# Attention pipeline of a transformer block: three batches' cross and self passes in 32 shared slots

## The reference, cut to what matters

```python
x = x + self_attention(norm(x))      # 16 heads, 4 key heads, width 32, ALiBi, window and global tokens masked out
x = x + cross_attention(norm(x), ctx, ctx)   # 32 heads, 8 key heads, width 16, keys = values = ctx
x = x + moe(norm(x))                 # 32 experts, top 4 of 2 groups, capacity 128, plus a shared expert
```

## Time and profile before

| | us |
|---|---|
| median of 3 runs (1155.79 to 1156.53) | 1156.13 |
| the profiled execution, its own time | 1159.79 |
| its span, first to last instruction | 1158.0 |
| busy in the span: PE / DVE / ACT / POOL | 1004.4 / 583.8 / 332.2 / 214.3 |
| mean granted clock of TensorE | 0.877 |

### The profile page before, as it was taken

How to read it: one execution, slowest core, us unless ns; L and a number is a source line. 1 busy time by engine, 2 the same in 40 slices (tenths; PEclk the granted TensorE clock), 3 DMA queues, 4 the chain that set the end, 5 groups by cost and what they waited for, 6 DMA issues and landing times.

```text
span 1158.0 us, 15121 instructions
## 1 busy us (share of the span) xinstructions
PE 1004.4 (87%) x5745; PEld 532.4 (46%) x5784; DVE 583.8 (50%) x1296; ACT 332.2 (29%) x639; POOL 214.3 (19%) x212
## 2 busy tenths in 40 slices
PE   2666898998998998998999798897999999999983
PEld 1535445545545545545535444233444444444441
DVE  1335836857857857857866947723122222222221
ACT  3021064154154154154164143161111111111110
POOL 6001001002102102102102203004322232322222
PEclk9678589689689689689589999698999999999997
DMA  6402202302302302302302404008277776777782
GB/s 214 133 2 73 56 2 74 92 2 74 92 3 74 92 3 73 92 3 73 92 3 74 129 2 128 2 1 291 47 182 211 210 208 215 221 185 218 209 231 33
DMA packets 95579, 119.26 MB, mean 103 GB/s; under 512 B 11185, under 2 KB 72049, under 8 KB 95504
## 3 DMA queue, kind: packets, MB, share of 16 engines
q1 hardware_dynamic: 80644, 96.52, 26.7%
q0 software_dynamic: 11408, 18.64, 8.2%
q10 hardware_dynamic: 3456, 3.15, 0.9%
HBM read 70.90 MB, written 21.07 MB: 79 GB/s over the span
## 4 chain that ended last, share of the span: by engine, by line
PE 71%; DVE 14%; DMA 4%; ACT 4%; issue 3%; POOL 2%; SPq 0%; ACTq 0%; POOLq 0%; DVEq 0%
PE qa L1393 9%; PE qx L1143 5%; PE qa L1257 5%; PE pt L1362 5%; DVE mxx L868 5%; PE qx L1381 4%; PE vb L1210 4%; ACT arena L540 4%; PE qa L1088 4%; PE vb L1037 4%; PE qx L1037 4%; PE qx L1199 3%; PE qa L1118 3%; PE qa L1037 3%; PE va L1057 3%
## 5 line engine op out<-in xcount | busy, mean ns | idle before, releaser
L540 ACT ACTIVATE arena<-qx 128x512 f32<-128x512 f32 x268 | 151.2, 597 | 309.7 <-PE qx L1199 187.4
L868 DVE TENSOR_REDUCE mxx<-qx 128x2 f32<-128x512 f32 x256 | 166.3, 684 | 45.1 <-PE qx L1143 42.8
L1143 PE MATMUL qx<-arena 96*128 96x256 bf16 x512 | 120.6, 344 | 31.4 <-DVE mxx L868 30.9
L435 POOL TENSOR_TENSOR rstd<-mv,power 128x2 f32<-128x2 f32 x24 | 16.9, 702 | 651.6 <-DVE mv L732 651.6
L540 ACT ACTIVATE arena<-qa 128x512 f32<-128x512 f32 (+2 forms) x116 | 63.9, 553 | 217.3 <-PE qa L1393 95.6
L1393 PE MATMUL qa<-arena 128*128 128x512 f32 x256 | 115.2, 593 | 0.8 <-ACT arena L540 0.8
L1199 PE MATMUL qx<-arena 98*128 98x512 bf16 x256 | 98.9, 428 | 8.4 <-ACT arena L540 5.6
L528 POOL DMA_INDIRECT out<-arena,iw x32 | 50.4, 1576 | 209.4 <-DVE arena L997 137.0
L1210 PE MATMUL vb<-arena 128*32 128x256 f32 x1024 | 87.6, 416 | 1.8 <-ACT arena L540 1.1
L1143 PEld LDWEIGHTS qx<-arena 96*128 96x128 bf16 x512 | 41.5, 113 | 91.7 <-DVE mxx L868 74.6
L1118 PE MATMUL qa<-ks,qs 100*128 100x128 f32 x256 | 76.3, 451 | 7.7 <-DMA qs<-arena 7.7
(11 more groups left out here) (172 smaller groups left out, 1425.6 us busy)
## 6 DMA issues: line engine op xcount, KB each, us to landing
arena<-in_L_ffn_w SPq DMA_DIRECT2D x96, 512.0 KB, 6.0
qs<-arena SPq DMA_DIRECT2D x24, 384.0 KB, 5.0
arena<-arena SPq DMA_DIRECT2D x72, 128.0 KB, 2.4
res<-in_x SPq DMA_DIRECT2D x8, 512.0 KB, 9.0
xnd<-arena SPq DMA_DIRECT2D x8, 512.0 KB, 7.0
out<-res SPq DMA_DIRECT2D x8, 512.0 KB, 7.3
out<-res POOLq DMA_DIRECT2D x4, 1024.0 KB, 9.3
ks<-arena SPq DMA_DIRECT2D x48, 64.0 KB, 1.9
```

The source lines that it names most:

```text
L540: nc.scalar.activation(dst, src, func, **kw).then_inc(s[signal], 1)
L868: v_.reduce_max(mxx[:, col:col + 3:2], xbank[v % 2].rearrange("p (h n) -> p h n", h=2), AX.X).then_inc(s["x_max"], 1)
L1143: op = mm(xbank[v % 2][:, h * S:h * S + S], qxs[0:XSPLIT_ROWS, query_at(kv * 4 + half * 2 + h), t * P:t * P + P], kxs[1 - k % 2][0:XSPLIT_ ...
```

## The change

One loop over bodies k = -1 to 10, each of 32 slots. In slot j, TensorE does score unit j of batch k-1 (first pass), unit j-3 of the second pass of batch k-2 (the last three units of a batch fall in the next body, as k-3), and at the slots named by the constants the second self pass, projection and context of batch k, the gate of batch k-3, and norm, keys, queries and self scores of batch k+1. VectorE reduces score unit j of batch k-1, then does its share of the other batches; ScalarE does exp of unit j-3 and its share. The first pass uses one bank (`first_bank`), the second another (`second_bank`). `qxs` is doubled, `kxs` is loaded in halves of heads, the context is loaded twice a batch, the residual `res` becomes a ring of five batches with late loads of x, and the base rows of the shared expert are staged in the ring. Nine chunks of the shared expert stand in bodies 8 to 10 (`TAIL_CHUNKS`), three ahead of the experts, 20 are spread. The gather ring is 8 instead of 5, and the first two experts' weights are loaded in body 9.

```diff
+FETCH = 8
+RING = 5
+CHUNKS, FIRST_SPREAD, CHUNK_SPAN = 32, 12, 26
+TAIL_CHUNKS = {(8, 10): 0, (8, 22): 1, (9, 8): 2, (9, 20): 3, (10, 7): 4, (10, 9): 5, (10, 13): 6, (10, 16): 7,
+               (10, 18): 8}
+LEAD_CHUNKS = (9, 10, 11)
...
+def expert_of(i):
+
+    return (i - FIRST_SPREAD) * CHUNK_SPAN // (CHUNKS - FIRST_SPREAD)
...
-        xbank = [qx[:, 0:512], qx[:, 512:1024]]
-        quad = abank + xbank
-        duo = [qa, qx]
-        xo_bank = [va[:, :], va[:, :], pt[:, :]]
-
-        names = """const_in const_moved const_ready clear x_in w_in ffn_in gate_up_in ctx_in
+        first_bank, second_bank = qx[:, 0:512], qx[:, 512:1024]
...
-        AT_QUERY = (-1, -1, -1, 1)
-        AT_CONTEXT, AT_THIRD, AT_LOGITS = 7, 11, 14
-        AT_SELF = (23, 25, 27, 29, 30, 31)
-        LEAD = 5
-        AT_OUT, AT_NORM, AT_FIRST = 19, 23, 28
...
+        BODIES = range(-1, B + 3)
+        OFF = 3
+        AT_STATS, AT_OUT1, AT_NORM3, AT_WEIGHTS = (0, 1, 2), 6, (7, 8), 10
+        AT_KEYED, AT_WEIGH, AT_HEADS = 3, (6, 8, 10, 12), (7, 9, 11, 13)
+        AT_PROJECT, AT_ADD, AT_APPLY2 = (14, 15), (15, 16), 18
+        AT_BACK1, AT_THIRD, AT_LOGITS, AT_LOGITS_BACK = 5, (11, 12), (14, 15), 17
+        AT_CONTEXT, AT_CONTEXT_REM, AT_CONTEXT_LOW = 16, 18, 19
+        AT_FIRST, AT_NORM, AT_SPLIT = 17, 19, (20, 21)
+        AT_KEYS, AT_QUERY, AT_VALUES, AT_BACK0 = 20, (20, 21, 21, 22), 22, 23
+        AT_KEYS_LOW, AT_SCALED, AT_QUERY_LOW, AT_OUT0, AT_CHOOSE = 21, 23, 24, 24, 25
+        AT_COUNT, AT_SLOTS, AT_SELF = 27, 30, (28, 28, 29, 29, 30, 30, 31, 31)
+        AT_XN1, AT_SUMS, AT_XN3, AT_XT3, AT_GL, AT_TH = 4, (5, 6, 7), 9, 13, 16, 17
+        AT_KP, AT_XT, AT_KVOUT, AT_QH, AT_VS = (17, 19), 18, 20, 23, 23
...
-            for n, (place_, value) in enumerate(((qxs[96:P], 0.0), (kxs[0][96:P], 0.0), (kxs[0][96:98], 1.0),
-                                                 (kxs[1][96:P], 0.0), (kxs[1][96:98], 1.0))):
-                pool.wait_ge(s["clear"], n + 1)
-                nc.gpsimd.memset(place_, value).then_inc(s["clear"], 1)
-            pool.wait_ge(s["clear"], 6)
+            cleared = 1
+            for r in range(2):
+                for place_, value in ((qxs[r][96:P], 0.0), (kxs[r][96:P], 0.0), (kxs[r][96:98], 1.0)):
+                    pool.wait_ge(s["clear"], cleared)
+                    nc.gpsimd.memset(place_, value).then_inc(s["clear"], 1)
+                    cleared += 1
...
+            for k in BODIES:
+                if has(k - 2):
+                    sp.wait_ge(s["x_rows"], k - 1)
+                    go(qxs[k % 2][96:97], nxh[:], "xshift_in")
+                    go(qxs[k % 2][97:98], nxl[:], "xshift_in")
+                if has(k):
+                    sp.wait_ge(s["m_rows"], k + 1)
+                    go(qs[100:101].bitcast(F32), nmh[:].bitcast(F32), "shift_in")
+                    go(qs[101:102].bitcast(F32), nml[:].bitcast(F32), "shift_in")
+                if k == B - 1:
+                    sp.wait_ge(s["q_t"], B)
+                    go(sg_s, sg.rearrange("(c p) n -> p c n", p=P), "gate_up_in")
+                if k == B:
+                    sp.wait_ge(s["wo_done"], B * 2)
+                    go(su_s, su.rearrange("(c p) n -> p c n", p=P), "gate_up_in")
+                    go(sd_s, sd.rearrange("(c p) n -> p c n", p=P), "gate_up_in")
+                if has(k - 1):
+                    if k >= 3:
+                        sp.wait_ge(s["xst_unit"], (k - 2) * XU)
+                    sp.wait_ge(s["c_split"], k)
+                    key_half(k - 1, 1)
+                    query_half(k - 1, 1)
+                if has(k):
+                    if has(k - 2):
+                        sp.wait_ge(s["vx_ready"], k - 1)
+                    context_in(k)
+                if has(k - 3):
+                    sp.wait_ge(s["xn3"], k - 2)
+                    go(xnd[(k - 3) * S:(k - 2) * S].rearrange("(t p) d -> p t d", p=P),
+                       xn3.rearrange("p (t d) -> p t d", t=2), "xnd_out")
+                    if k > 3:
+                        sp.wait_ge(s["x2_out"], (k - 3) * 16)
+                    go(out_rows[:, k * 2 - 6:k * 2 - 4], tokens(k - 3), "x2_out")
+                if has(k - 1):
+                    if has(k):
+                        sp.wait_ge(s["c_t"], k + 1)
+                    elif has(k - 2):
+                        sp.wait_ge(s["vx_ready"], k - 1)
+                    context_in(k - 1)
+                if k + 2 in late_in:
+                    sp.wait_ge(s["x2_out"], (k - 2) * 16)
+                    sp.dma_start(tokens(k + 2), rows[:, 2 * k + 4:2 * k + 6]).then_inc(late_in[k + 2], 16)
+                if has(k):
+                    sp.wait_ge(s["c_split"], k + 1)
+                    if has(k - 2):
+                        sp.wait_ge(s["xst_unit"], (k - 2) * XU + XU // 2)
+                    key_half(k, 0)
+                    query_half(k, 0)
+                if has(k + 1):
+                    sp.wait_ge(s["k_split"], k + 2)
+                    for m, part in enumerate((kh, kl, kh)):
+                        for blk, j0 in enumerate((P, GLOB)):
+                            go(ks[m:SPLIT_ROWS:3, blk].bitcast(F32), part.bitcast(F32)[:, j0:j0 + P], "ks_in")
+                    sp.wait_ge(s["q_hi"], k + 2)
+                    go(qs[0:SPLIT_ROWS:3].bitcast(F32), qh.bitcast(F32), "qs_in")
+                    go(qs[1:SPLIT_ROWS:3].bitcast(F32), qh.bitcast(F32), "qs_in")
+                    sp.wait_ge(s["q_split"], k + 2)
+                    go(qs[2:SPLIT_ROWS:3].bitcast(F32), ql.bitcast(F32), "qs_in")
+                if k == B + 1:
+                    sp.wait_ge(s["qxs2_in"], B * 96)
+                    sp.wait_ge(s["kxs2_in"], B * 96)
+                    expert_in(0)
+                    expert_in(1)
...
+            def cross_max(b, v):
+                kv, t, half = v // 4, v // 2 % 2, v % 2
+                dve.wait_ge(s["xs_unit"], b * XU + v + 1)
+                if v == 0:
+                    dve.wait_ge(s["xm_t"], b)
+                col = t * XH + query_at(kv * 4 + half * 2)
+                v_.reduce_max(mxx[:, col:col + 3:2], first_bank.rearrange("p (h n) -> p h n", h=2), AX.X
+                              ).then_inc(s["x_max"], 1)
...
+            dve.wait_ge(s["const_ready"], 1)
+            for k in BODIES:
+                for j in range(XU):
+                    if has(k - 1):
+                        cross_max(k - 1, j)
+                    if has(k + 1):
+                        if j == AT_STATS[0]:
+                            if k == -1:
+                                dve.wait_ge(s["x0_in"], 16)
+                            elif k + 1 < RING:
+                                dve.wait_ge(s["x_in"], (RING - 1) * 16)
+                            else:
+                                dve.wait_ge(late_in[k + 1], 16)
+                            norm_tile(1, k + 1, 0)
+                        if j == AT_STATS[1]:
+                            link(norm_tile(1, k + 1, 1))
+                        if j == AT_STATS[2]:
+                            norm_stats(1)
+                        if j == AT_WEIGHTS:
+                            token_weights(k + 1)
+                    if has(k - 3):
+                        if j == AT_OUT1:
+                            cross_out(k - 3, 1)
+                        if j == AT_NORM3[0]:
+                            norm_tile(3, k - 3, 0)
+                        if j == AT_NORM3[1]:
+                            link(norm_tile(3, k - 3, 1))
+                            norm_stats(3)
+                    if has(k):
+                        if j in AT_HEADS:
+                            heads_out(k, AT_HEADS.index(j))
+                        if j in AT_ADD:
+                            project_out(k, AT_ADD.index(j))
+                        if j == AT_APPLY2:
+                            norm_apply(2, k, xn2)
+                        if j == AT_CONTEXT_REM:
+                            context_rem(k)
+                        if j == AT_CONTEXT_LOW:
+                            context_low(k)
+                        if j == AT_SPLIT[0]:
+                            dve.wait_ge(s["n_t"], k + 1)
+                            v_.tensor_copy(xp[0], pt[:]).then_inc(s["n_hi"], 1)
+                            dve.wait_ge(s["n_hi"], k + 1)
+                            v_.tensor_tensor(xr, pt[:], xp[0], ALU.subtract).then_inc(s["n_rem"], 1)
+                        if j == AT_SPLIT[1]:
+                            dve.wait_ge(s["n_rem"], k + 1)
+                            v_.tensor_copy(xp[1], xr).then_inc(s["n_mid"], 1)
+                            dve.wait_ge(s["n_mid"], k + 1)
+                            v_.tensor_tensor(xp[2], xr, xp[1], ALU.subtract).then_inc(s["n_split"], 1)
+                    if has(k + 1):
+                        if j == AT_KEYS_LOW:
+                            keys_low(k + 1)
+                        if j == AT_SCALED:
+                            queries(k + 1)
```

(129 more changed lines are left out.)

1129 lines of the change are left out of this document (435 added, 694 removed).

## The result

The changed kernel takes **1256.38 us** (median of 4 runs, 1255.67 to 1257.40) where the kernel before, on the same chip, took 1156.33. The ratio is **1.0866**, 95% interval 1.085 to 1.0883: slower by 100 us. The profiled execution has a span of 1254.7 us, 96.7 more than before.

A forecast was written before the change was run, and what follows sets the result against it. It took TensorE and VectorE, neither full, to bound the kernel by waiting on each other. Counts at 884.5, plus 28 and 316, gave a 1228.5 us span, called 1226 us; range 1115 to 1262, the forecast's own 1190 to 1260.

The forecast's parts named there:

- rival A: Overlap works, a body gets near VectorE's list: 74 us a body, 1117 us in all; chance 0.25.
- Start +6.9: At the start, a second clearing of 32 partitions on POOL delays the first statistics by 6.9 us.
- Bodies 0, 1, 2: 134.5, then 80 and 82: Filling bodies: body 0 ends at 134.5 us, body 1 takes 80 and body 2 takes 82.
- A full body 90: Slot-by-slot sum of 86 us at full clock, 25 with TensorE idle, plus 4 for half clock.
- VectorE's list, 67.5: VectorE's work in one body, reduces and shares, summed to 67.5 us; perfect overlap would give 68.
- Clock 4 us a body, bounds 0 and 12: Half clock in slots 28 to 31 and the next body's first slots costs 4 us, between 0 and 12.
- Five full bodies 450: Bodies 3 to 7, all counted as full, take 450 us.
- Body 8: 64, bodies 9 and 10: 27 + 47 = 74: Last bodies: body 8 takes 64 us, body 9 47, body 10 up to the counts 27, chunks included.
- Counts to the first expert 28, then 316: Last counts to first expert transposes 28 us; then the experts 316, the floor of the adds' chain on POOL.
- Rival B: Short idles in every slot keep the clock down: a body of 98 us, 1280 us in all; chance 0.08.
- Rival C: DMAs of the splits come late each body: +5 us a body, 1260 us; no separate chance.
- My rule, 614 + 6.8 x body: Whole time as 614 + 6.8 x body length; 1156 us is met at a body of 79.8 us.

The follow-up runs named there:

- experiment 5: Changed kernel without the clearing of the second query buffer: 1263.15 us, ratio 1.0806.
- Experiment 1: Changed kernel with the choice of experts cut from one piece behind unit 25 into six behind units 20 to 26: 1230.82 us, ratio 1.0624.
- kernel 9: Experiment 1 plus filling matmuls that nobody reads behind units 25 to 27 and 0 to 2: 1218.80 us, ratio 1.0534.
- experiments 9 and 10: The first is kernel 9; the second has spread choice, three banks, no clearing and filling matmuls, against the same without filling: 1207.50 us, ratio 1.0426.
- Experiment 4: Changed kernel with the nine shared-expert chunks moved from the last three bodies to in front of the experts: 1288.13 us, ratio 1.1126.
- Experiment 11: Filled kernel with spread choice, three banks, no clearing, plus two banks in turn for the last batch's second pass: 1197.34 us, ratio 1.0325.
- kernels 3 and 8: Changed kernel with three banks for first-pass units 25 to 31: 1240.20 us, ratio 1.0709; the same with spread choice and no clearing: 1226.52 us, ratio 1.0603.
- experiment 7: Changed kernel with spread choice, three banks, cut projections, keys and queries, query rows prepared one slot later, no clearing: 1234.29 us, ratio 1.0572.
- kernel 12: Experiment 11 plus the output projection's eight pieces cut over slots 11 to 15, keys and queries left: 1173.60 us, ratio 1.0125.

## Why the prediction was right, and where it was off

The forecast of slower held, 1226 against 1256, inside the forecast's own range of 1190 to 1260, and rival A (overlap that works) did not come. That it lies inside owes something to errors that cancel: up to the end of body 7 the sum was 12.6 us too long, in the last three bodies 41 too short. Term by term:

- *Start +6.9.* Measured 7.0, and experiment 5 gave 7 us back.
- *Bodies 0, 1, 2: 134.5, then 80 and 82.* Measured 132.0, 78.4, 82.2. TensorE's wait for the self scores' transfer, bared in body 0, is there (9.9 us the longest).
- *A full body 90.* Measured 92.4, 87.6, 88.3, 92.8, mean 90.3. The steps under it hold: a wait of 6.49 us behind the choice where I gave slots 23 to 27 their 15.1 us; VectorE idle 5.3 us under the projections (I had said 6 to 8); half clock after the wait. Experiment 1 shows the first by removing it (5 us a body). The full-clock sum of 86 can be read off too: kernel 9, clock 1.00, has 81.7 with the choice spread, so 86.7 with its 5 us, an estimate.
- *VectorE's list, 67.5.* Its items as written add up to 75, and the traces have VectorE busy 61 us. The slot sum doesn't use it; only the argument for rival A did.
- *Clock 4 us a body, bounds 0 and 12.* 3.2 to 5.3 by experiments 9 and 10, with the choice spread. In the changed kernel itself filling gave 2.2 us a body and brought the clock to no more than 0.90 to 0.92; from the estimate of 86.7 it would be 3.6.
- *Five full bodies 450.* Measured 441.3: body 7 took 80.2, not 90. I had counted it as full although it has no next batch: the wrong row, since the earlier trace rows has just such a body at 5 us less.
- *Body 8: 64, bodies 9 and 10: 27 + 47 = 74.* Measured 76.8 and 102.6. **This is the term that failed**, 41 us. Experiment 4 splits it. Without any chunk these bodies take 64.5 and 78.5. The forecast without its chunks is 38 + 14 = 52 for body 8, and at most 35 + 27 = 62 for bodies 9 and 10 (five chunks stood inside the 27 with no price of their own). So at least 29 of the 41 us lie in the bodies themselves. The chunks cost 12.3 us in body 8, where I had 11.5, and 24.1 in bodies 9 and 10, where I had 12 and what was in the 27. The step that failed is the price of their rounds, taken at the full clock. In its place the rows show a clock of 0.74 in body 8 and 0.82 in 9 and 10 (0.66 and 0.61 without chunks); in body 8 TensorE waiting for reduces 14.4 us in 15 waits, the longest 6.5 behind the choice; in bodies 8 to 10 a bank from which each exponential must come out first (12.3 us in 18 waits), and 7.0 us at the end for the last choice. Experiment 11 took 7.8 us back through the bank alone, and filling in body 8 gave 1.7 (73.6 to 71.9, kernel 1 to 9). Filling in bodies 9 and 10 was not tried, so how the rest divides between clock and waits stays open.
- *Counts to the first expert 28, then 316.* Measured 28.6 and 312.8. That the chain of adds is the floor there was not tried.
- *Other signs.* The first pass of batch 0 starts at 130.3 where I said near 135. The first expert transposes come at 941.9, not near 912: the 41 us of the last bodies, less what the earlier ones came out shorter.

Rival B, cold for good, did not come; the clock swings between its two levels, 1.00 and 0.50 in the windows above. I had cited the Trainium skill (TensorE: Matmul & The Clock Gate, section A second HAM failure mode: psum-queue depth-cycling) for it, but that section says only that short idles make the clock swing, not that it stays down, so it was no ground for B. The traces agree with the swinging. With the source they agree in part: with filling matmuls in the idle places the clock of a full body was 0.94 to 1.00, but kernels 3 and 8, which idle less than kernel 1, were no warmer (0.81 to 0.85 against 0.83 to 0.91). Rival C did not come with the change; experiment 7 made it, 2.3 to 3.7 us a body, by preparing the queries one slot later when nothing longer hid them.

What I had not said is the plainest reading: a batch takes 85.8 us in both kernels. The waits moved from one place to another, a whole body grew by 3.6 us, the bodies with less work made up for that, and the price was one more body to fill and a longer drain. My rule, 614 + 6.8 x body, is too steep and its constant too small: kernel 1 has bodies 5.1 us shorter and took 26 us less, kernel 9 8.3 and 38, so 4.5 to 5 us for each; and kernel 12 with bodies of 80.1 would have 1159 by it and took 1174.

## What to carry to other kernels

Before deepening a pipeline, compute the period from the slot list with each engine's longest in-order lump: a lump that sits whole in one slot (here 6.5 us of small VectorE operations) stalls every unit behind it, whatever the depth, while the depth itself costs a whole body at each end. With eight batches, each us of the mean period is worth 7 us, so the two ends (116 us here, 97 with what the experts gave back) want a period 14 to 17 us shorter. Look at whole bodies too: a mean over bodies with more and less work hid here that the whole ones had become longer. Take out the longest wait first, then look at the clock: once waits are gone the same idle stretch can return as work at half speed.

## What the runs showed of the hardware

- A TensorE at half clock stayed there for 24 us while the records show it busy 21.11 of them (experiment 3), and the same program has bodies of 0.81 and of 0.89 side by side. Its busy time in a record is no sign that the clock will return.
- Extra work made the kernel faster: 30 matmuls a body that nobody reads took 12 us off the time (kernel 1 to 9, 1230.82 to 1218.80 us; 10 by the ratios).
- A chunk in front of the experts costs 69.9 / 9 = 7.8 us on average (experiment 4), though the matmuls of the nine hold only some 48 us at the full clock (an estimate, 5 x 6.9 + 4 x 3.4). Between the up chunks there TensorE waits for VectorE's product of the one before, 12.8 us in six waits, and in five of the first ten windows of some 10 us the clock was 0.70 to 0.83.
